# Attention stage: both last blocks of values in one group behind beat 3, the sums at beat 9, the scaling behind beat 13

## What is computed

```python
def _L1_xattn_ref(q, k, v):          # q: normed x, k = v = ctx; b=16, h=8, d//h=32
    qh = q.reshape(b * h, d // h, m)
    kh = k.reshape(b * h, d // h, -1)
    vh = v.reshape(b * h, c // h, -1)
    qk = jnp.einsum('bdm,bdn->bmn', qh, kh) * scale
    sm = jax.nn.softmax(qk, axis=-1)
    ret = jnp.einsum('bmn,bcn->bcm', sm, vh)
...
x = x + jnp.tanh(g_xattn[1]) * _L1_xattn_ref(_layernorm(x, axis=-1), ctx_2048, ctx_2048)
x = x + jnp.tanh(g_ffn[1]) * _L1_ffn_ref(_layernorm(x, axis=-1), L1_ffn_w_router, L1_ffn_w_fc, L1_ffn_w_proj)
```

## Time and profile before

| what | us |
|---|---|
| median of 3 runs | 1590.01 (1587.80 to 1590.67) |
| profiled execution | 1588.79 |
| its span | 1587.0 |
| TensorE busy | 1493.7 (94%) |
| VectorE busy | 1195.8 (75%) |
| ScalarE busy | 960.5 (61%) |
| GpSimd busy | 1018.1 (64%) |
| mean granted TensorE clock | 0.979 |

### The profile page before, as it was taken

How to read it: one execution, slowest core, us unless ns; L and a number is a source line. 1 busy time by engine, 2 the same in 40 slices (tenths; PEclk the granted TensorE clock), 3 DMA queues, 4 the chain that set the end, 5 groups by cost and what they waited for, 6 DMA issues and landing times.

```text
span 1587.0 us, 28309 instructions
## 1 busy us (share of the span) xinstructions
PE 1493.7 (94%) x8801; PEld 1072.7 (68%) x8801; DVE 1195.8 (75%) x1964; ACT 960.5 (61%) x1497; POOL 1018.1 (64%) x791
## 2 busy tenths in 40 slices
PE   4999999998889699999999999898999999999996
PEld 4677777776555554444444444588999999998995
DVE  7688888888927778888888885384777777777774
ACT  6433323232924178888888887645777667776773
POOL 4788888885504588888888887303555555555553
PEclk9999999999989799999999999999999999999998
DMA  7244443443764787878887781662444444444443
GB/s 262 85 145 145 146 143 133 144 145 85 213 129 161 184 204 193 208 200 211 210 206 203 204 200 58 233 249 50 76 77 80 80 76 73 79 80 79 72 77 53
DMA packets 114972, 224.27 MB, mean 141 GB/s; under 512 B 17088, under 2 KB 17088, under 8 KB 113984
## 3 DMA queue, kind: packets, MB, share of 16 engines
q1 hardware_dynamic: 98400, 185.10, 40.8%
q0 software_dynamic: 15904, 37.23, 13.2%
q10 hardware_dynamic: 576, 0.79, 0.2%
HBM read 146.71 MB, written 75.84 MB: 140 GB/s over the span
## 4 chain that ended last, share of the span: by engine, by line
PE 33%; DMA 24%; issue 4%; DVE 3%; POOL 2%; ACT 1%; SPq 0%; ACTq 0%; POOLq 0%; DVEq 0%
DMA out_rows<-XN,slots 22%; PE pB L1458 9%; PE pA L1444 7%; PE pO L1468 7%; PE pB L1478 4%; DMA XN<-normed_rows,slots 1%; PE pB L112 1%; PE pB L1616 1%; POOL out_rows L1426 1%; PE pA L1604 1%; DMA qs<-turned 1%; PE pA L1521 1%; PE pO L1616 1%; PE pA L1528 1%; PE pB L1537 0%
## 5 line engine op out<-in xcount | busy, mean ns | idle before, releaser
L1795 DVE TENSOR_REDUCE low<-pA 128x2 f32<-128x1024 f32 x256 | 303.2, 1218 | 64.1 <-PE pA L1444 64.1
L436 PE MATMUL y<-kv,toep 128*128 128x288 f32 x1280 | 327.8, 413 | 9.0 <-DVEq L63 5.8
L1426 POOL DMA_INDIRECT out_rows<-XN,slots x71 | 197.0, 2775 | 215.5 <-DMA out_rows<-XN,slots 173.5
L1686 ACT ACTIVATE pt<-pB 128x512 f32<-128x512 f32 x512 | 277.8, 601 | 57.4 <-PE pB L1458 53.2
L436 PEld LDWEIGHTS y<-kv,toep 128*128 128x128 f32 x1280 | 239.1, 191 | 97.5 <-DVEq L63 34.1
L1604 PEld LDWEIGHTS pA<-XN,fc 128*128 128x128 f32 x2272 | 265.5, 192 | 10.9 <-issue 5.6
L1604 PE MATMUL pA<-XN,fc 128*128 128x128 f32 x2272 | 266.4, 276 | 5.0 <-DVE XN L1960 4.0
L1458 PE MATMUL pB<-qs,ks 98*128 98x512 f32 x512 | 213.9, 431 | 1.1 <-ACT pt L1686 0.7
L406 ACT ACTIVATE ym<-y 128x384 f32<-128x384 f32 (+1 forms) x128 | 52.6, 411 | 230.6 <-PE y L436 230.6
L1444 PE MATMUL pA<-ks,qs 96*128 96x512 f32 x512 | 184.3, 402 | 4.7 <-DMA qs<-q_low 3.2
L1458 PEld LDWEIGHTS pB<-qs,ks 98*128 98x128 f32 x512 | 96.9, 190 | 131.9 <-ACT pt L1686 79.5
(11 more groups left out here) (294 smaller groups left out, 2481.8 us busy)
## 6 DMA issues: line engine op xcount, KB each, us to landing
ks<-ctx_high SPq DMA_DIRECT2D x62, 256.0 KB, 4.9
qs<-q_high SPq DMA_DIRECT2D x62, 256.0 KB, 7.0
kc<-in_ctx_conv SPq DMA_DIRECT2D x32, 384.0 KB, 5.4
XN<-in_x SPq DMA_DIRECT2D x16, 512.0 KB, 9.8
toep<-kernel_and_skip SPq DMA_DIRECT2D x32, 256.0 KB, 3.5
ct<-in_ctx SPq DMA_DIRECT2D x16, 512.0 KB, 6.3
ctx_high<-kh SPq DMA_DIRECT2D x16, 512.0 KB, 4.4
ctx_low<-kl SPq DMA_DIRECT2D x16, 512.0 KB, 5.1
```

Of the source, the lines that this page charges most:

```text
L436: m = pe.matmul(y[half].rearrange("p (l n) c -> p l n c", l=CB)[:, l, :, 0:PAIRS], toep[u][:, (l - s) * P:(l - s + 1) * P], kv[u][:, half, ...
L1426: pool.indirect_dma_start(out=out["out"], out_offset=bass.IndirectOffsetOnAxis(ap=slots[:, j:j + 1], axis=0), in_=ys[j % 2], in_offset=Non ...
L1686: act.activation(pt[s][:, h, :], pB[n % 3], ACT.Exp, scale=SCALE1).then_inc(s_exp, 1)
L1795: dve.tensor_reduce(low[u % 2][:, 2 * n:2 * n + 2], pA[n % 2], op=ALU.max, axis=AX.X, negate=True).then_inc(s_red, 1)
```

## The change

In the beats of TensorE, the values of blocks 2 and 3 of the unit before are both issued behind beat 3; block 3 stood behind beat 11. The sums move from beat 7 to beat 9 (the constant SUM, which also sets the bank they use and the place of the logarithm). ScalarE's `inverse` moves from behind exponential 10 to behind exponential 11, VectorE's `scale` from behind the reduction of beat 11 to behind that of beat 13. EARLY_AT, LEAD and the number of instructions stay.

```diff
-        SUM = 7
+        SUM = 9
...
                     if beat == 3 and exists(j - 1):
                         values(*before, 2)
-                    if beat == 11 and exists(j - 1):
                         values(*before, 3)
...
-                        if k == 10 and exists(j - 1):
+                        if k == 11 and exists(j - 1):
                             inverse(j - 1)
...
-                    if beat == 11 and exists(j - 1):
+                    if beat == 13 and exists(j - 1):
                         scale(j - 1)
```

## The result

The changed kernel takes 1652.15 us (median of 4 runs, 1649.87 to 1660.39), the kernel before 1588.9 in the same comparison: ratio 1.0407, 95% interval 1.0385 to 1.0428. Two executions that stand far apart from the others of their kernels, 1711.02 us of the kernel before with half the reduction and 2969.74 us of the three double groups, are left out of the ratios further down. The profiled execution has a span of 1651.2 us, 64.2 more than before.

A forecast was written before the change was run, and what follows sets the result against it. TensorE's order, 14.06 us a unit, was taken as the bound. 1588.8 + 51.6 (29 units at 1.78 more) + 2.4 (last two units) = 1643 us; range 1618 to 1656, chance 0.84.

The forecast's parts named there:

- The two waits: TensorE: score 8 ahead of the sums waits for a reduction, 0.57 us lost; values wait for the scaling, 1.51 lost.
- The merge gains 0.36: TensorE's groups: two single groups become one double, saving 0.15, one lead-in and one long first step, 0.36 us a unit.
- The rival in which only the merge is seen: Reductions end early enough, no waits: 0.44 us a unit gained, 13 us in all, 1576 us; chance 0.05.
- Before the sums: Stretch from beat 4 to the sums: score 8 waits for beat 5's reduction, 0.57 us lost, plus 0.10 long step.
- Behind the sums: Beats 9 to 15: three reductions, then the scaling, hold the values until 5.00 us behind beat 9, 1.51 us lost.
- The rival with only the ring of banks: Scaling not in the way; score 14's wait puts the values 4.36 us behind beat 9, 1624 us; chance 0.13.
- The unit: One pass of TensorE's attention loop: 15.86 us against 14.08, 1.78 more; 51.6 us over 29 units.
- The last two units: Units 30 and 31, paced by ScalarE at 13.05 us: about 14.3 each, 1.2 more each, 2.4 for both.
- What moves at no cost: ScalarE's logarithm, exponentials and inverse, GpSimd's partial sums and SyncE's transfers: relaxed by a longer unit, costed at nothing.
- The thinnest cover: Before the sums, ScalarE's exponential 6 ends near 6.8 us and its bank is wanted at 7.16: 0.3 us spare.
- The signs: Profile marks: unit near 15.9, named waits, reductions and scaling back to back, double group 1.85, TensorE busy some 87%.
- The fourth rival: TensorE's clock falls to half for one 14-matmul stretch a unit: 3.2 us a unit, 1700 us or more; chance 0.03.

The follow-up runs named there:

- the kernel before with half the reduction: The kernel before, with VectorE's reduction over only half of each score's keys, so the output is not the reference's: 1589.19 us, ratio 0.9995.
- the three double groups: Changed kernel with sums at beat 8, scores 9 and 14 reordered, scaling behind beat 11, inverse behind exponential 10, normalising behind exponential 7: 1597.52 us, ratio 1.0044.
- the two variants above: The kernel before with only the sums moved to beat 9, 1616.84 us; the changed kernel with reductions over half of each score's keys, 1606.37 us.

## Why the prediction was right

The two waits and their sizes came as predicted; the stretches of the unit agree with the walk within 0.04 us. The time itself, 1652.15, is 1 us outside the spread that the forecast gave for itself (1633 to 1651) and inside the range named at the end (1618 to 1656). What it is above 1643 is not of the predicted mechanism: it is mostly the half-clock groups below, which the sum had at nothing.

- *The merge gains 0.36.* The double group takes 1.86 us as before (754.61 to 756.47), so by the rows the saving is in every unit. No run shows it by itself: where the groups were merged, another wait came each time. The rival in which only the merge is seen fell with the merge alone (unit 14.58).
- *Before the sums.* b4 to b9 was put at 9.01 less 3.93, 5.08; it is 5.04 (744.56 to 749.60). The kernel with the sums at 9 alone shows the wait of score 8 without the other changes.
- *Behind the sums.* b9 to the values was put at 5.00 and is 5.01, and the scaling's part of it, 0.64, measured 0.68 (5.01 less 4.33). The rival with only the ring of banks is what the kernel with the scaling at 11 is: 4.33 for 4.36.
- *The unit.* 15.86 against 15.85; 29 units 51.6 against 51.8.
- *The last two units.* 1.2 each; 1.1 in the last, and in unit 30 also 1.2 once its half-clock group (3.23 us for 1.92) is taken off.
- *What moves at no cost.* It held in the changed kernel. The thinnest cover, ScalarE's before the sums, was named, and it failed in the two variants above, by 0.30 and 0.35 us. It is thinner than the 0.3 us of the prediction: in both variants the sums start about 0.22 behind the end of exponential 6, so in the changed kernel, where that ends near 747.39 and the sums start at 747.74, some 0.13 is left (an estimate from these rows).
- *The signs.* One did not come: TensorE's busy share was to fall to some 87% and is 92% (427.89 of 466.23). A matmul counts as busy for 0.39 to 0.50 where a step is 0.235, so part of each wait is hidden: s8 is 0.54 late and the profile shows 0.39 idle.
- *The clock.* Here a size was off. The fourth rival took a whole stretch of every unit at the lower level, 3.2 us a unit, or nothing. (At that level a step takes 0.43, 553.67 to 554.10 in the kernel before, and not the 0.46 of the prediction, so it would have been 2.7.) What came is one group in four of 29 units and one in unit 30, 8 us together. With the 2.1 us outside the stage that is the distance from 1643 to the profiled execution, 1652.9; where these 2.1 come from is open.

Two readings of rows were loose. Unit 0 does have one group, the values behind its last beat (560.53); the wait at 559.39 comes before it and is read rightly. And the 0.94 us that the prediction sets beside VectorE's 1.13 is the time of full-array multiplications: it shows that VectorE is slower than TensorE at a pair, and no run here shows what tiling does to either.

What the prediction costed at nothing is only just so behind VectorE: ScalarE is the next bound of this order. With the reduction at 0.69 us the unit is still 14.55, so the sentence that the other three engines have 2 us to spare is true of ScalarE only as a mean.

## What to carry to other kernels

Merging two small groups saves a fixed price (0.36 us here by the rows: 1.85 in place of 2.00, one lead-in and one long first step), but a group can also be the time in which another engine catches up: before a group is taken out, look whether between the filling of every bank of a short ring and its next use there is still one. With two banks of pairs, eight pairs and reductions that take 1.13 us to TensorE's 0.94, four groups cover all pairs; by count three cover at most six, since one group lies in no more than two of these gaps. An operation that the next group waits for should not be put behind one more piece of a queue that is already late: from beat 11 to beat 13 the scaling's place cost 0.7 us a unit, since the values were held up by score 14 anyway, and from 13 to 15 a full reduction, 1.15.

## What was not expected of the hardware

Behind a wait of TensorE of 0.62 to 0.64 us by the profile (1.0 from start to start where 0.33 is ordinary) the granted clock fell to half for one group now and then. In the changed kernel the four long groups start at 608.63, 721.25, 833.86 and 946.45, that is 112.6 us apart each time, and each time it is the group right behind the wait. With the scaling at 11, where that wait is gone and others of 0.39 us stay, there is none in these units. With the wait of 1.78 us in every unit (scaling at 15) there are five in 29, no more than that. The wait for the scaling is not needed for it: in unit 30 of the changed kernel (1041.64) and of the three double groups (986.29) it is a group behind a wait of about 0.5 us for ScalarE, while in the kernel before the clock stayed at 1.00 behind 0.80 us. Why it is these units stays open; no run here tells it.
